# A decoder layer on one core: VectorE's order around the value block's first sum in the retention heads, and four low parts by accumulating transfers

## The reference, cut to what matters

```python
q = _rope((x @ Wq).reshape(B, T, 8, 128)); k = _rope((x @ Wk).reshape(B, T, 8, 128))
v = (x @ Wv).reshape(B, T, 8, 256);        g = (x @ Wg).reshape(B, T, 8, 256)
scores = einsum('bihd,bjhd->bhij', q * scale, k) * D        # D: decay, causal
o = einsum('bhij,bjhd->bihd', scores, v)
o = o * rsqrt(mean(o * o) + eps) * g_norm_weight * (g * sigmoid(g))
x = _layernorm(x + o.reshape(B, T, 2048) @ Wo)
...
x = _layernorm(x + xattn(x, ctx))                           # its wv gives the value weights
...
x = _layernorm(x + ffn(x))
```

## Time and profile before

| | us |
|---|---|
| median of three runs | 2631.72 |
| the profiled execution | 2630.63 |
| its span, first to last instruction | 2628.8 |
| TensorE matmul busy | 2593.5 (99%) |
| VectorE busy | 1814.5 (69%) |
| ScalarE busy | 1197.4 (46%) |
| GpSimd busy | 20.7 (1%) |

### The profile page before, as it was taken

One profiled execution on the slowest core, in us unless ns is written; L12 is line 12 of the kernel. 1 busy time (PEld: TensorE's weight loads), 2 busy tenths in 40 slices (PEclk: granted clock), 3 DMA queues, 4 the chain that ended last, 5 costly groups with the idle time before them and its releaser, 6 DMA issues.

```text
span 2628.8 us, 41662 instructions
## 1 busy us (share of the span) xinstructions
PE 2593.5 (99%) x16328; PEld 2456.2 (93%) x16328; DVE 1814.5 (69%) x2506; ACT 1197.4 (46%) x2043; POOL 20.7 (1%) x33
## 2 busy tenths in 40 slices
PE   9999999999999999999999999999999999999998
PEld 9999999989999998898889999889998999999997
DVE  7777776677777774867788888736973763763766
ACT  6555555554444443344466666522531431431441
POOL 0000000000000000000000000000000000000000
PEclk9999999999999999999999999999999999999999
DMA  5444445422222231144256666421121121211121
GB/s 197 160 145 161 149 135 180 146 71 63 61 72 62 78 90 51 63 105 92 77 143 175 174 168 166 107 72 57 48 81 48 65 81 49 81 65 65 65 80 51
DMA packets 138188, 262.68 MB, mean 100 GB/s; under 512 B 25012, under 2 KB 98220, under 8 KB 125100
## 3 DMA queue, kind: packets, MB, share of 16 engines
q1 hardware_dynamic: 136108, 255.53, 30.9%
q0 software_dynamic: 1920, 4.92, 1.1%
HBM read 198.24 MB, written 57.26 MB: 97 GB/s over the span
## 4 chain that ended last, share of the span: by engine, by line
PE 91%; DVE 6%; issue 2%; ACT 1%; DMA 0%; DVEq 0%; SPq 0%; ACTq 0%
PE PS L3666 6%; PE PS L3664 6%; PE PS L3668 6%; PE PS L3137 5%; PE PS L135 4%; PE PS L133 4%; PE PS L134 4%; PE PS L3150 3%; PE PS L1167 3%; PE PS L1169 3%; PE PS L1171 3%; PE PS L1130 3%; PE PS L1132 3%; PE PS L1134 3%; PE PS L3702 3%; PE PS L3701 3%
## 5 line engine op out<-in xcount | busy, mean ns | idle before, releaser
L3807 ACT ACTIVATE WH<-RAW 128x512 fp32r<-128x512 f32 x180 | 113.4, 631 | 222.2 <-PE PS L3668 119.8
L133 PE MATMUL PS<-XH,WH 128*128 128x512 f32 (+1 forms) x592 | 204.2, 345 | 1.0 <-DVE WL L99 1.0
L135 PE MATMUL PS<-XH,WL 128*128 128x512 f32 (+1 forms) x592 | 204.4, 345 | 0.0
L4048 DVE TENSOR_TENSOR WL<-RAW,WH 128x512 fp32r<-128x512 f32 x196 | 134.7, 688 | 58.5 <-ACT WH L3807 55.2
L134 PE MATMUL PS<-XL,WH 128*128 128x512 f32 (+1 forms) x496 | 170.1, 343 | 0.0
L3666 PE MATMUL PS<-XL,WH 128*128 128x400 f32 x480 | 166.0, 346 | 0.0
L3664 PE MATMUL PS<-XH,WH 128*128 128x400 f32 x480 | 164.8, 343 | 0.8 <-issue 0.6
L3668 PE MATMUL PS<-XH,WL 128*128 128x400 f32 x480 | 165.0, 344 | 0.0
L3309 DVE TENSOR_TENSOR XL<-PS,XH 128x400 fp32r<-128x400 f32 (+2 forms) x224 | 122.6, 571 | 56.5 <-ACT XH L3242 51.6
L3242 ACT ACTIVATE XH<-PS 128x400 fp32r<-128x400 f32 (+2 forms) x224 | 106.3, 507 | 96.1 <-PE PS L3150 96.0
L1726 ACT ACTIVATE WH<-RAW 128x512 fp32r<-128x512 f32 x132 | 81.5, 632 | 117.6 <-DVE RAW L2025 66.5
(11 more groups left out here) (535 smaller groups left out, 8162.8 us busy)
## 6 DMA issues: line engine op xcount, KB each, us to landing
RAW<-weights_dram SPq DMA_DIRECT2D x100, 1024.0 KB, 4.9
values_scratch<-VS SPq DMA_DIRECT2D x44, 512.0 KB
a_KHL<-keys_scratch SPq DMA_DIRECT2D x32, 411.0 KB, 5.1
RAW<-context_dram SPq DMA_DIRECT2D x6, 2048.0 KB, 8.7
XH<-values_scratch SPq DMA_DIRECT2D x16, 640.0 KB
XL<-values_scratch SPq DMA_DIRECT2D x16, 640.0 KB
R<-context_dram SPq DMA_DIRECT2D x4, 2048.0 KB, 9.2
keys_scratch<-KS SPq DMA_DIRECT2D x16, 512.0 KB, 3.8
```

What stands on the lines that cost most here:

```text
L133: pe.matmul(out, wh, xh[:, k, cols], start=(k == 0), stop=False)
L135: mm = pe.matmul(out, wl, xh[:, k, cols], start=False, stop=(k == KT - 1))
L4048: dve.tensor_tensor(ring[1][:, e % RING, :], src, ring[0][:, e % RING, :].bitcast(F32), ALU.subtract).then_inc(f_lo, 1)
```

## The change

Four edits, all in written order or in who does the work; no product, sum or transfer of the heads is added or taken away.

1. In heads 1 to 6 VectorE does `combine(i, 1, "u2")` directly behind the low part of product 3 of the value block, ahead of the queries' cosine, of a mix and of their sine. The second low part of the earlier head's output (`output_lo(i - 1, 1)`) moves from in front of product 2's low part to behind `u2`, `combine(i, 0, "c21")` comes ahead of the first such part, `mix(i, 1, 3)` ahead of product 5's low part, and the queries' sine behind that.
2. The low part (and on ScalarE the high part) of output entry 1 moves ahead of the rotated queries' split.
3. In head 1 `mix(1, 1, 1)` moves ahead of `gated_output(0)`.
4. `values_lo(v)` is gone. ScalarE writes minus the high part into the low part's tile right behind each high part (`minus_hi`), and GpSimd adds the raw unit to it by an accumulating transfer of 512 KB, one at a time (`add_raw`), and posts `c.w_lo` itself.

```diff
+def minus_hi(c, act, lo, raw):
+    act.activation(lo, raw, ACT.Copy, scale=-1.0).then_inc(c.minus, 1)
+def add_raw(c, pool, n, lo, raw, landed, by=1):
+    pool.wait_ge(c.minus, c.MINUS + n + 1)
+    pool.dma_start(lo, raw, accum_op=ALU.add).then_inc(c.sum_in, 16)
+    pool.wait_ge(c.sum_in, 16 * (ROPE_SUMS + n + 1))
+    pool.sem_inc(landed, by)
...
+            pool.wait_ge(c.w_lo, U_V)
+            for v in range(KV_N):
+                add_raw(c, pool, v, c.VW[:, v, 1, :], raw_unit(c, U_V + v), c.w_lo)
...
                 act.activation(c.VW[:, v, 0, :], raw_unit(c, u), ACT.Copy).then_inc(c.w_hi, 1)
+                minus_hi(c, act, c.VW[:, v, 1, :], raw_unit(c, u))
...
                 output_entry_hi(i, 0)
+                output_entry_hi(i, 1)
                 rotated_hi(i, 0)
-                output_entry_hi(i, 1)
...
                     mix(i, 1, 0)
+                    mix(i, 1, 1)
                     gated_output(i - 1)
                 product_lo(i, 1, 0)
-                if i == 1:
-                    mix(i, 1, 1)
                 mix(i, 1, 2)
                 product_lo(i, 1, 1)
+                combine(i, 0, "c21")
                 output_lo(i - 1, 0)
-                combine(i, 0, "c21")
-                output_lo(i - 1, 1)
                 product_lo(i, 1, 2)
                 combine(i, 0, "c12")
                 product_lo(i, 1, 3)
+                combine(i, 1, "u2")
+                output_lo(i - 1, 1)
+                product_lo(i, 1, 4)
                 rotate_cos(i, 0)
-                product_lo(i, 1, 4)
+                mix(i, 1, 3)
+                product_lo(i, 1, 5)
                 rotate_sin(i, 0)
-                mix(i, 1, 3)
-                combine(i, 1, "u2")
-                product_lo(i, 1, 5)
                 combine(i, 1, "u3")
                 combine(i, 1, "c22")
                 product_lo(i, 1, 6)
                 output_entry_lo(i, 0)
+                output_entry_lo(i, 1)
                 rotated_lo(i, 0)
                 rotate_cos(i, 1)
                 rotate_sin(i, 1)
-                output_entry_lo(i, 1)
                 combine(i, 1, "c21")
                 output_entry_lo(i, 2)
                 add_output(0, i)
...
-                if n == 2 or n == 5:
-                    values_lo(n // 3)
...
-            values_lo(2)
-            values_lo(3)
             norm.refine(dve, 0)
...
             copy_value(0)
+            dve.wait_ge(c.w_lo, U_V + KV_N)
             split_lo(c, dve, U_V + 4)
```

More of the change, by code:

```diff
@@ L67 @@
 PAIRS = U_END // 2
+ROPE_SUMS = 4 * (RH - 2)
 class Core:
@@ L1282, in phase_context @@
         done.wv_mix = wv_mix
+        c.minus, c.MINUS = wv_hi, 8
         done.K_STORED = [k_stored_by(GROUPS) for _ in range(2)]
@@ L1559, in phase_retention @@
         s_raw, S_RAW = before.wv_mix, 4
+        c.sum_in = rope_in
         f_hi, F_HI = before.k_sq, 8 * GROUPS
@@ L2123, in end_lo @@
                                   ALU.subtract).then_inc(c.w_lo, 1)
[L2125 to L2129, removed]
             def add_last(h, n):
```

## The result

The changed kernel takes 2662.88 us (median of 4 runs, 2661.02 to 2664.58) against 2631.47 for the kernel before beside it: ratio 1.0119, 95% interval 1.0102 to 1.0137. The forecast was 2636 us, and at most 2641.5. The profiled execution took 2662.75, with a span of 2661.0, 32.2 longer than before.

What follows compares the result with a forecast made beforehand. TensorE, busy for 99% of the span, bounds the kernel. Heads 2 to 6 5.0 us slower, head 1 1.1 faster, load 1.3 slower, seam 1.0 faster: 4.2 slower, 2636 on the median; range 2628.5 to 2641.5.

Steps and rivals of the forecast that it cites:

- The first sum, removed wait: Heads 1 to 6: with `u2` earlier product 3's wait goes, 1.04 us a head, 5.2 in five; head 1 2.4.
- the new wait of head 1: Head 1: `mix(1, 1, 1)` ahead of the gated output delays product 0's low part, a new wait of about 0.7 us.
- What is late next, the sine: Heads 2 to 6: sine 3.3 us later, so output tile 2 waits (7.3 in all) and tile 5 once (2.4).
- the formula T - 3.84: Output tile 2, heads 2 to 6: its wait, T being GpSimd's issue to ScalarE's split; 1.5 us at the mean.
- A load beside the trip: Heads: SP's next weight pair runs beside the queries' trip, 0.2 us added each, six times, 1.3 slower.
- the weight pair slows the trip by its full 1.2: Rival, queries' trips: the load costs each the whole 1.2 us, 6 x 1.0 on top, 2642; chance 0.18.
- the floor of 2628.6: Rival, heads: all trips take 4.6 us, tile 2 costs 0.9 in five heads, tile 5 nothing; chance 0.20.
- The value weights: Seam: VectorE loses four subtractions, 1.0 us faster; transfers of 512 KB, taken as 5.3 each, are in time.
- `add_output(0)` isn't held: Rival, heads: chain wrong or trip's tail hidden; first sums give 5.2 + 3.0, seam 1.0, 2622.5 us; chance 0.06.

Runs made afterwards that it cites:

- seam-only kernel: The kernel before with only the value weights' low parts made by accumulating transfers, the heads' order left old: 2629.41 us, ratio 0.9994.
- e7_gap_shift: Changed kernel with rotation directly behind `u2` and SP's loads held until trips end, plus a norm constant loaded by GpSimd's queue instead of SP's: 2622.17 us.

## Why the prediction was wrong

**The first sum, removed wait: right.** Product 3 follows product 2 without a wait in every head, and the new wait of head 1, forecast at 0.7, is 0.5.

**What is late next, the sine: right in mechanism and chain.** Releaser, place (tile 2 in each head, tile 5 in head 2) and the steps on either side of the trip (4.10 between `u2` and the sine, 5.96 for 5.88 from the split to tile 2) came as written. With the loads held, the waits at tile 2 are 1.46, 0.92, 0.89, 0.97, 2.23 and 2.57; the forecast had 1.7 in head 1 and 1.5 in the others, each with 0.11 of restart. The mean of the last five, 1.5, agrees, in part by luck: it rests on one trip with the gap and one of 6.16 that nothing forecast. Tile 5 waits 1.45 in head 2 (forecast 2.4) and, not forecast, 1.08 in head 4. In the changed kernel itself the formula T - 3.84 gives 2.95 for head 2's trip of 6.79, and the wait was 2.86.

**A load beside the trip: the term that failed.** The prediction put it at 0.2 us a trip, 1.3 in all, with 1.2 a trip as the upper bound, "since a load moves no data in its first microseconds". When the pair is issued it had right (1.5 us behind GpSimd's issue, as measured). The queries' pairs, the only ones that it priced, cost 20.2 us; the keys' pairs, which are issued 2.7 to 2.8 us into their trips in place of 3.6 to 5.3, and for which it had no term, cost 6.9. Together that is 27.1 for 1.3, too small by a factor of twenty. Without this term the forecast was some 2634.7, and with the loads held the kernel measures 2635.75, so the rest of the sum held. Four parts of it were wrong:
- Its reason. The load has no data-free first microseconds: in the kernel before, the pair's first bytes came 0.9 us behind its issue. Issued 1.5 us into a trip of 4.8, it has bytes to move for the last 2.4 us of it.
- Its size per trip. The queries' trips grew by 2.9 in the mean (7.7 for 4.8 without the gap). The upper bound assumed that the last 1.2 us of a trip could at worst be doubled. But the second of the two transfers had all its data still to move, and the load has 1024 KB where it has 200. The strip of the changed kernel shows it: until 656.0 some 195 KB had moved, the first transfer alone, and from 656.3 to 660.9 the second shares the engines with the load, with a dip near 657.
- Its multiplier. Tile 2 had no slack left, as the prediction itself had found, so every microsecond of trip was paid in full by TensorE. Tile 5 of head 2, forecast at 2.4 for a keys' trip of 7.1, waited 4.49 for one of 9.52.
- What a wait brings with it. The forecast gave a restart of 0.11. Five of seven waits were followed by some 3 us at the lower clock. Changed against held, busy time is 6.2 longer and the waits are 30.3 - 11.6 = 18.7 longer: together 24.9, where the two profiled spans differ by 25.0.

The rival "the weight pair slows the trip by its full 1.2" named this very place and had 0.18, but with the same wrong bound; so even the range's end, 2641.5, was taken from a bound that no row carried. The kernel with half a pair shows how far off it was: 512 KB alone cost 1.5 a trip. Smaller slips don't matter here: six times 0.2 is 1.2 and not 1.3, and the floor of 2628.6 leaves the load's 1.3 out.

**The value weights: right.** By the starts of the same matmuls at both ends of the seam TensorE gains 1.0 there in the changed kernel and in the seam-only kernel alike (the time of the latter can't tell it from nothing), and the transfers take 5.1. The Trainium skill's fit (DMA: Bandwidth & Descriptors, Anatomy of one DMA — SWDGE (gpsimd) path), from which the prediction estimated 3.2 us, is below what was measured here for a transfer that adds 512 KB from SBUF into SBUF: 5.1 from issue to issue, and a median of 4.5 from issue to landing over the four transfers of the seam-only kernel. The measurement decides.

**The other rivals.** "`add_output(0)` isn't held" had 2622.5 for the case that the trip is hidden: the sine directly behind `u2` with held loads makes that case, and measures 2622.15. The sum 5.2 + 3.0 + 1.0 of that rival stands, 9.2 for 9.1 measured.

**Whether VectorE's work lengthens a trip.** The prediction left this aside under the floor, as no row separated such trips. Two kernels now do. Here are the queries' trips of head 2 with the loads held, and with the sine first and the loads held (columns as in the stretches above; the third pair is VectorE's busy time):

```profile
648.28:653.14 4.86, 4.86 (x29) 4.86 (x28) 2.57 (x5) 0.63 (x1) 1.63 (x2) 1.00 0.51 84
644.01:648.80 4.79, 4.79 (x29) 4.79 (x28) 4.69 (x9) 1.79 (x3) 1.62 (x2) 1.00 0.52 86
```

VectorE works for 2.57 us of the one and 4.69 of the other, and both trips take 4.8 to 4.9. The first four queries' trips of the two kernels are 4.71 to 5.00 and 4.78 to 4.85. So the trips aren't shorter where VectorE stands idle.

## What to carry to other kernels

When an instruction that starts a transfer moves later, look at what the other queues issue in the microseconds behind it, and price an overlap by bytes: here 1 MB issued 1.5 us behind two transfers of 200 KB made their trip 3 us longer in the mean, 2.8 us behind mostly a few tenths where the two were issued without the gap, and 4.0 us behind nothing (4.7 to 4.9). Where nothing hides the trip, hold the load by a wait on the trip's end if its data can wait; here they could. A wait of TensorE of some microseconds is not priced by its length alone: look at the granted clock behind it.

## What the hardware showed that was not expected

- A load on SP's queue and transfers on GpSimd's slow each other: 4.6 for 3.5 us to landing on the one side and 6.5 for 5.2 on the other in head 2. Half the load made about half the excess (7.7, 6.2 and 4.8 us in the mean).
- Five of the seven new waits of TensorE (2.68 to 6.25 us) were followed by 3 us at a granted clock of 0.50 to 0.52, in which 8 matmuls ran in place of 16; one of 3.98 was followed by 0.66. One of 2.86 was not: clock 1.00. In the kernel with the loads held, waits up to 1.5 us left it at 1.00, and those of 2.23 and 2.57 were followed by 0.71 and 0.59. With half a pair, one of 2.02 was followed by 0.70 and one of 3.23 by 1.00. Length alone doesn't separate these cases; no run here tells what does. The rows of these four, two with the loads held and two with half a pair:

```profile
881.80:884.80 3.00, 3.00 (x12) 2.69 (x13) 2.43 (x4) 0.00 (x0) 0.00 (x0) 0.71 0.63 108
957.64:960.64 3.00, 3.00 (x10) 2.51 (x11) 2.44 (x4) 0.00 (x0) 0.00 (x0) 0.59 0.63 110
...
663.00:666.00 3.00, 3.00 (x12) 2.69 (x13) 2.44 (x4) 0.00 (x0) 0.82 (x1) 0.70 0.61 114
973.03:976.03 3.00, 3.00 (x16) 2.59 (x17) 2.97 (x5) 0.00 (x0) 0.00 (x0) 1.00 0.88 163
```

- GpSimd's issue gap of 2.5 us has a fixed place in the sequence of its transfers, the same in every kernel here but one, whatever their timing, and one transfer more ahead of them, with its two waits, moved it.
- The trips of 6.16 (queries, head 5) and 5.98 (keys, head 4) with the loads held have no weight pair issued from 4 us ahead of them until they are over. Both have a transfer of instructions in them, one packet of 0.02 MB. The DMA queues from 869 to 877 us, around the trip of 6.16 (slices of 0.2 us):

```profile
DMA  0000000000949969496899320001100000000009
...
q8 instruction: 1, 0.02, 1.2%
```

The bulk has moved by 873.8, and a trickle goes on to 875.0. The same packet is in all six trips over 5.4 us that have neither the gap nor a pair's data beside them (5.65 before and 5.65 in the seam-only kernel, these two, and 5.78 and 5.45 in `e7_gap_shift`). But five such trips with the packet took 4.8 to 5.05, so what makes it cost something stays open. The 6.48 of the changed kernel, the longest of its keys' trips without the gap, has the packet as well.
